# Gated cross attention and mixture of experts on one core: two x buffers, search rounds and masks placed anew between the shared units, and low weight parts of the first pieces made on TensorE

## What is computed

```python
# attention part
Q, K = h @ Wq.T, h @ Wk.T                         # h = ctx
sim = einsum('bhnd,bhmd->bnm', Q, K) / (sqrt(32) * 4)
thr = the 153rd largest value of each row of sim
A = sigmoid(sim) * (sim >= thr); A = (A + A.T) / 2
x = x + tanh(g0) * ((1 - gamma) * layernorm(x) + gamma * A)
# feed-forward part
n = layernorm(x)
shared = silu(n @ gate.T) * (n @ value.T) @ down.T        # 704 hidden columns
scores = sigmoid(n @ gate_w.T); the 2 best of 8 experts by scores + bias, weights normalised
out = x + tanh(g1) * (shared + sum over the two experts of w_e * expert_e(n))   # 352 hidden columns each
```

## Time and profile before

| | |
|---|---|
| median of 3 runs | 589.0 us |
| profiled execution | 588.87 us |
| its span, first to last instruction | 587.1 us |
| PE busy | 494.9 us (84%) |
| DVE, ACT, POOL busy | 343.4, 263.1, 231.5 us |
| mean granted TensorE clock | 0.934 of full speed |
| granted clock from 25 to 50 us, and from 50 to 75 us | 0.51 and 0.64 |

### The profile page before, as it was taken

The page is one execution under the profiler, slowest core; times in us unless marked ns, Lnnn a source line. Parts: engine busy times, 40 slices in busy tenths (PEclk is TensorE's granted clock), DMA queues, the critical chain, the costliest instruction groups (busy, mean ns, idle before and its releaser), DMA issues.

```text
span 587.1 us, 10965 instructions
## 1 busy us (share of the span) xinstructions
PE 494.9 (84%) x3105; PEld 275.4 (47%) x3106; DVE 343.4 (58%) x708; ACT 263.1 (45%) x473; POOL 231.5 (39%) x226
## 2 busy tenths in 40 slices
PE   2402588879996999778998899999999999999992
PEld 0100343334442444334464566666666666666661
DVE  0589758787868796977993577433333333333331
ACT  1696578736784569524141265322223223222221
POOL 2147835463344524470133034433443443443422
PEclk9855769989998999896999999999999999999998
DMA  3236293204720482025005589454454355345333
GB/s 117 95 85 181 79 303 118 58 18 172 263 57 19 143 291 58 20 73 185 1 0 157 189 222 258 89 91 89 73 88 91 71 82 96 72 78 98 73 40 49
DMA packets 32048, 63.73 MB, mean 109 GB/s; under 512 B 4048, under 2 KB 4304, under 8 KB 32016
## 3 DMA queue, kind: packets, MB, share of 16 engines
q1 hardware_dynamic: 23280, 42.89, 22.5%
q0 software_dynamic: 8736, 20.45, 19.3%
HBM read 41.05 MB, written 22.28 MB: 108 GB/s over the span
## 4 chain that ended last, share of the span: by engine, by line
PE 56%; DVE 18%; ACT 9%; issue 7%; DMA 5%; POOL 2%; SPq 1%; DVEq 1%; POOLq 0%; ACTq 0%
PE py L1021 13%; PE pg L1001 12%; PE pu L1002 12%; PE pg L860 4%; PE pu L860 4%; PE pt_bank L818 4%; DVE w L1195 3%; DVE pa L1154 3%; DVE w L1125 2%; PE pa L1011 2%; ACT w L627 2%; ACT w L633 2%; PE pu L880 1%; DVE w L1158 1%; DVE w L1202 1%
## 5 line engine op out<-in xcount | busy, mean ns | idle before, releaser
L1001 PE MATMUL pg<-w,x_t 128*128 x468 | 140.7, 313 | 0.0
L1002 PE MATMUL pu<-w,x_t 128*128 x468 | 140.7, 313 | 0.0
L555 POOL DMA_INDIRECT out<-rows,idx x39 | 61.8, 1584 | 141.5 <-ACT rows L758 131.4
L1021 PE MATMUL py<-w,work 128*128 x351 | 82.1, 379 | 0.8 <-DVE work L1453 0.8
L860 PE MATMUL pg<-w 128*128 128x512 f16 x288 | 78.2, 388 | 2.4 <-DVE work L1249 2.4
L748 ACT ACTIVATE work<-pg 128x352 f32<-128x352 f32 x39 | 18.1, 464 | 132.1 <-PE pu L1002 132.1
L860 PE MATMUL pu<-w 128*128 128x512 f16 x240 | 66.7, 388 | 0.0
L594 ACT ACTIVATE w<-stage 128x544 f16<-128x544 f32 (+1 forms) x80 | 50.8, 648 | 34.3 <-DMA stage<-in_weights 33.8
L496 POOL TENSOR_TENSOR w<-stage,w 128x544 f16<-128x544 f32 (+1 forms) x43 | 53.5, 1254 | 27.2 <-ACT stage L598 25.3
L1442 DVE SCALAR_TENSOR_TENSOR work<-pu,work 128x352 f32<-128x352 f32 x39 | 20.5, 525 | 62.6 <-ACT work L748 62.5
L1001 PEld LDWEIGHTS pg<-w,x_t 128*128 128x128 f16 x468 | 45.8, 98 | 20.5 <-issue 0.6
(11 more groups left out here) (199 smaller groups left out, 800.4 us busy)
## 6 DMA issues: line engine op xcount, KB each, us to landing
stage<-in_weights SPq DMA_DIRECT2D x80, 272.0 KB, 3.6
w<-in_x SPq DMA_DIRECT2D x4, 1024.0 KB, 6.8
out<-w SPq DMA_DIRECT2D x16, 256.0 KB, 2.8
xn_rows<-w SPq DMA_DIRECT2D x16, 256.0 KB, 4.9
out<-rows SPq DMA_DIRECT2D x13, 256.0 KB, 3.2
rows<-out SPq DMA_DIRECT2D x12, 256.0 KB, 3.3
w<-in_ctx_t SPq DMA_DIRECT2D x4, 256.0 KB, 3.5
out<-rows,idx POOLq DMA_INDIRECT x39, 4.8
```

The source lines that it names most:

```text
L555: pool.indirect_dma_start(out=out, out_offset=bass.IndirectOffsetOnAxis(ap=idx[:, t:t + 1], axis=0), in_=rows[:, t % 2, :], in_offset=None ...
L1001: pe.matmul(pg[p][:, 0:H], lhs, w[:, item, half, at:at + H], start=begin, stop=end)
L1002: mm = pe.matmul(pu[p][:, 0:H], lhs, w[:, item, half, at + H:at + 2 * H], start=begin, stop=end)
L1021: mm = pe.matmul(py[:, :], hid_t[:, p, part * JC + j, :], w[:, item, half, at:at + C], start=(j, part, half) == (0, 0, 0), stop=(j, part) ...
```

## The change

All of these are made together.

- **Two x buffers** (`xbs`), one for even and one for odd batches, and a buffer `kept` for the masked scores, all in the space of weight item 6. The new x stays in its buffer until the shared rows are added; the store and reload of x are gone.
- **x in one step.** ACT's `base` and POOL's adds are gone. DVE does x = x * gain + kept (scalar_tensor_tensor, four per batch) and then adds the transpose and the shift in one instruction.
- **Masks** are written without waiting for the missed counts, behind the products of units 3 and 4; the check (`check`) follows unit 5's. `a_made` counts batches instead of tiles.
- **Search.** Rounds 0, 1 and 2 are issued ahead of unit 0's product, and round 3 behind it; x statistics move from before the search to behind unit 2's product (for batch 0 ahead of the score statistics).
- **Low parts on TensorE.** For pieces 0 to 5 PE multiplies the stage slot with `W_SCALE` times the identity and the high part with minus the identity, in two halves of 272 columns, and ACT copies each half out of PSUM.
- **Pieces.** 10 pieces are made before the rows of batch 0, the other shared and first expert pieces in slots behind the units: 0, 1, 2, 2, 2, 3 of them in each period and 2, 2, 2, 2 behind units 0 to 3 of the last batch. POOL makes the low parts of pieces 6 to 47, DVE those of the late ones. The shared weights lie in flat order (groups, then down parts), and in batch 0 each unit waits only for the pieces that it reads.
- **Rows.** Statistics and row scalars go by halves of two tiles. ACT copies turned tiles 1 and 3, behind tanh; DVE copies 0 and 2, behind the four score statistics and a shared row. For batch 0, ACT writes the high part directly and DVE makes the exact row itself.
- The loops over periods are unrolled.

```diff
-BEFORE = 3
-FIRST = 14
-BY_DVE = 20
+BY_PE = 6
+FIRST = 10
+SLOT_PIECES = (0, 1, 2, 2, 2, 3)
+PER_PERIOD = sum(SLOT_PIECES)
+LAST_PIECES = (2, 2, 2, 2, 0, 0)
...
-        xb = attn_tiles()
+        beside = w[:, EARLY - 1, :, :].rearrange("p b c -> p (b c)").bitcast(F32)
+        xbs = [beside[:, 0:TPB * SEQ].rearrange("p (i c) -> p i c", i=TPB), attn_tiles()]
+        kept = beside[:, TPB * SEQ:2 * TPB * SEQ].rearrange("p (i c) -> p i c", i=TPB)
...
             def together(b, more):
-                base_scalars(b + 1)
+                slots = period_pieces(b)
                 for u in range(UPS):
+                    if u == TPB - 1:
+                        base_scalars(b + 1)
                     shared_low(b, u)
-                    if u < TPB:
-                        low_piece(b + BEFORE, u)
-                add_attention(b + 1)
-                for n in range(TPB, CHUNKS - 2):
-                    low_piece(b + BEFORE, n)
-                row_scalars(b + 1)
-                for n in range(CHUNKS - 2, CHUNKS):
-                    low_piece(b + BEFORE, n)
+                    for piece in slots[u]:
+                        low_piece(*piece)
+                row_scalars(b + 1, 0)
+                row_scalars(b + 1, 1)
...
             for u in range(UPS):
                 shared_low(BATCHES - 1, u)
+                for piece in period_pieces(BATCHES - 1)[u]:
+                    low_piece(*piece)
...
+            def low_from_banks(k):
+                at = k % CHUNKS * CHUNK_W
+                for half in range(2):
+                    after(act, low_mm, k * 2 + half + 1)
+                    act.activation(w[:, k // CHUNKS, 1, at + half * HALF_W:at + (half + 1) * HALF_W],
+                                   low_banks[low_pair(k)][half][:, 0:HALF_W], ACT.Copy).then_inc(w_lo[k % RING] if half else low_sb, 1)
...
-            def scores_and_rows(b, more, pieces=()):
-                if more:
+            def scores_and_rows(b, more):
+                if more and b:
                     keep_qk(b + 1)
-                for k in pieces:
-                    high_piece(k // CHUNKS, k % CHUNKS)
                 for i in range(TPB):
                     normalised(b, i)
                 if more:
                     keep_scores(b + 1)
-                after(act, up_mm, b * UPS)
-                after(act, xt_mm, (b + 1) * TPB)
-                act.activation(x_tb[:, :, (TPB - 1) * P:], xt_banks[(TPB - 1) % 2], ACT.Copy).then_inc(xt_act, 1)
-                if more:
                     score_tanh(b + 1)
+                rows_turned(b, 1)
+                rows_turned(b, 3)
...
             def together(b, more):
+                slots = period_pieces(b)
                 count(b + 1, 0)
                 keep_logits(b)
+                count(b + 1, 1)
                 for u in range(UPS):
                     shared_silu(b, u)
-                    if u + 1 < ROUNDS:
-                        count(b + 1, u + 1)
...
+                    if u == 0:
+                        count(b + 1, 2)
+                    if u in (1, 2):
+                        scaled_sigmoid(b + 1, 2 * u - 2)
+                        scaled_sigmoid(b + 1, 2 * u - 1)
+                    shared_high(b, u)
+                    if u == 0:
+                        count(b + 1, 3)
+                    for piece in slots[u]:
+                        high_piece(*piece)
...
+            def low_pieces(begin, end):
+                for k in range(begin, end):
+                    at = k % CHUNKS * CHUNK_W
+                    after(pe, w_hi, k + 1)
+                    for half in range(2):
...
+                        pe.matmul(bank_[:, 0:HALF_W], scaled_ident[:], stage[:, k % RING, lo:hi], start=True, stop=False)
+                        pe.matmul(bank_[:, 0:HALF_W], minus_ident[:], w[:, k // CHUNKS, 0, at + lo:at + hi],
+                                  start=False, stop=True).then_inc(low_mm, 1)
...
             pe.wait_ge(const_ok, 2)
+            low_pieces(0, RING)
             missed_rows(0)
+            after(pe, w_lo[RING - 1], 1)
+            turn_attention(0)
             project(1, None)
-            turn_attention(0)
+            low_pieces(RING, RING + 1)
             for i in range(TPB):
                 scores(1, i)
+            low_pieces(RING + 1, BY_PE)
             for i in range(TPB):
                 turn_batch(0, i)
-            for s in w_lo:
-                after(pe, s, HALVES * (CHUNKS // RING))
-            after(pe, w_hi, HALVES * CHUNKS)
...
+                after(dve, base_ok, b + 1)
+                for i in range(TPB):
+                    o.mark(dve.scalar_tensor_tensor(out=xbs[b % 2][:, i, :], in0=xbs[b % 2][:, i, :], scalar=pt[:, 4, i:i + 1],
+                                                    in1=kept[:, i, :], op0=ALU.mult, op1=ALU.add))
                 if shared is not None:
                     shared_rows(shared, 0)
                 for i in range(TPB):
-                    after(dve, xa_made, b * TPB + i + 1)
                     after(dve, at_mm, b * TPB + i + 1)
-                    dve.tensor_tensor(xb[:, i, :], turn_banks[i][:, :], xb[:, i, :], ALU.add).then_inc(x1_made, 1)
+                    o.wait()
+                    dve.scalar_tensor_tensor(out=xbs[b % 2][:, i, :], in0=turn_banks[i][:, :], scalar=pt[:, 5, i:i + 1],
+                                             in1=xbs[b % 2][:, i, :], op0=ALU.add, op1=ALU.add).then_inc(x1_made, 1)
...
             def together(b, more):
+                search(b + 1, 0)
+                if b:
+                    shared_rows(b - 1, TPB - 1)
+                search(b + 1, 1)
+                search(b + 1, 2)
+                shared_hidden(b, 0)
+                search(b + 1, 3)
+                last_counts(b + 1, (0, 1))
+                shared_hidden(b, 1)
+                thresholds(b + 1, (0, 1))
+                last_counts(b + 1, (2, 3))
+                thresholds(b + 1, (2, 3))
+                shared_hidden(b, 2)
                 x_stats(b + 1)
-                search(b + 1, 0)
...
+                shared_hidden(b, 3)
+                count_missed()
+                masks(b + 1, (0, 1))
+                shared_hidden(b, 4)
+                masks(b + 1, (2, 3))
+                shared_hidden(b, 5)
+                check(b + 1)
                 attended(b + 1, more, b)
```

More of the change, by code:

```diff
@@ L502, in shared_low @@
                 if u == MIXED:
+                    for n, low in enumerate(w_lo):
+                        after(pool, low, len(range(n, pieces_by(b, u), RING)))
                     after(pool, hlo_sb, q)
@@ new lines, in low_rows @@
+                def low_rows(i, made):
+                    after(dve, xn_hi, b * TPB + i + 1)
+                    if made is not None:
+                        o.wait(made)
+                    dve.tensor_tensor(xnr[:, i, C:2 * C], xn[:, i % 2, :], xnr[:, i, 0:C], ALU.subtract).then_inc(xn_lo, 1)
+                for i in (0, 2):
+                    if i and b == 0:
+                        after(dve, xn_lo, b * TPB + i)
+                    made = [exact(i), exact(i + 1)] if b == 0 else [None, None]
+                    low_rows(i, made[0])
+                    low_rows(i + 1, made[1])
@@ L1235, in attended @@
-                if more:
-                    score_stats(b + 1, (2, 3))
+                    rows_turned(b, 0)
+                    rows_turned(b, 2)
+                    if not more:
+                        shared_rows(shared, 3)
                 o.clear()
```

475 lines of the change are left out of this document (232 added, 243 removed).

## The result

The changed kernel takes 586.2 us (median of 8 runs, 583.9 to 587.5), the kernel before beside it 589.1 (588.4 to 591.1): the ratio on record, from all runs side by side, is 0.9937, 95% interval 0.9915 to 0.9958 (the two medians alone give 0.9951). It is faster by 0.5 to 0.6%, where 595.0, slower by 1%, had been forecast. The profiled execution took 586.68 us with a span of 584.8, 2.3 less than before.

The account below looks back on a forecast made before the run. PE carries 56% of the chain that ended last, with its waits for vector work on the path. The sum was 588.9 - 3.6 (front) + 0 (period 0) + 2.2 (period 1) + 2.4 (period 2) + 5.1 (last batch) = 595.0 us, range 582 to 602.

Parts of the forecast that it names:

- front: Before unit 0 of batch 0: earlier attention, most of it lost again behind low products and piece loads; 3.6 us gained.
- period 0: Batch 0's unit 0 to batch 1's: PE waits 6.4 us for a low piece before down products; 0 in the sum.
- period 1: Unit 0 of batch 1 to that of batch 2: middle gains 1 us, tail costs more; 2.2 us longer.
- period 2: Unit 0 of batch 2 to that of batch 3: normalising at 51.8 us, low clock in last down product; 2.4 longer.
- last batch: Unit 0 of batch 3 to the experts: eight Pool pieces hold DVE's one-hot work, partly covered by slack; 5.1 us longer.
- experts: Expert tiles at the end of the kernel: their 258 us are not touched, no term in the sum.
- the middle of periods 1 and 2: Unit 0 to normalising: masks leave PE's path, four x instructions join; normalising at 50.3 against 51.3 us, 1 us gained.
- The hold: Running Pool instructions delay DVE's four two-input x instructions, each by 1.15 us: 6.8 us instead of 2.6 free.
- The tail: Normalising to next unit 0: turned-tile copies stand behind score work; 12.4 to 13.0 us against 10.5, cost 2 to 2.5.
- rival 1: Periods gain because Pool's pieces miss the four x instructions, shown by new x by 41 us; 581 to 585, chance 0.22.
- rival 2: Last batch's hold mostly missed, as Pool's pieces fall on reductions and PSUM reads; 588 to 590.5 us, chance 0.14.
- the forecast's own 592 to 599: Whole kernel slower by the last batch's hold and the longer tail; chance 0.52.

Follow-up runs that it names:

- e10: e7 with Pool clearing instead of subtracting the low part of the seven pieces beside units 3 to 5 of each period: 575.2 us, ratio 0.9751.
- e2: Changed kernel with turned tiles copied ahead of tanh (ACT) and ahead of and between the score statistics (DVE): 581.6 us, ratio 0.9842.
- e1: Changed kernel with Pool's subtraction for the last batch's eight pieces replaced by a memset, leaving out item 5's low weights: 579.2 us, ratio 0.9798.
- e4: Changed kernel with batch 0's wait for all 16 shared pieces before the first down product replaced by a wait per unit: 579.8 us, ratio 0.9802.
- e9: Changed kernel with pieces 0 to 5 made by ACT and Pool as before the change, without identity products on PE: 583.4 us, ratio 0.9895.
- e3: Changed kernel with Pool's three subtractions of each period's last slot moved behind the row scalars: 590.0 us, ratio 0.9976.
- e5: Changed kernel with the masks of batches 1 to 3 behind the check again, ahead of the x scaling: 592.8 us, ratio 1.0053.
- e6: Changed kernel with the edits of e2, e3 and e4 together: 580.3 us, ratio 0.9848.
- e7: Changed kernel with the edits of e2 and e4 together, Pool's pieces not moved: 579.7 us, ratio 0.9838.
- e8: e7 with six of the last batch's eight pieces moved into the three periods: 575.5 us, ratio 0.9742.

## Why the prediction went wrong, step by step

The terms of the sum against the stage table, in us against the kernel before:

| term | predicted | measured |
|---|---|---|
| front | -3.6 | -4.7 |
| period 0 | 0 | -0.1 |
| period 1 | +2.2 | -1.3 |
| period 2 | +2.4 | -1.4 |
| last batch | +5.1 | +4.7 |
| experts | 0 | +0.6 |
| sum | +6.1 | -2.3 |

**The step that failed is the middle of periods 1 and 2.** The two terms were 3.5 and 3.8 us too high, 7.3 of the 8.4 that the sum missed. They made a loss of 2.2 and 2.4 us out of what became a gain of 1.3 and 1.4, and with it the sign of the whole. The mechanism was as told, its sizes were not.

- Period 1, in us behind the start of its unit 0: the x instructions start at 35.6 (predicted 36.7) and take 5.6 (6.8); the new x starts at 41.8 (44.2); ACT normalises at 47.4 (190.00 in the trace) where 50.3 was said. The hold was priced at 4.2 us over the free 2.6, as if each of the four met a Pool instruction; it is 3.0, which is three at 1.6 us and one free at 0.74 (the row below has both prices), and e10 took 1.95 of it away. The 1.1 us of the start is a chain ahead of unit 2's product that was placed 1.2 us too late (20.6 measured, 21.8 told). The rows behind the new x took another 0.5 us less than said.

```profile
L1260 DVE SCALAR_TENSOR_TENSOR w<-w,pt x16: 739/1602/1702, 48.9 to 243.2; 128x512 f32<-128x512 f32 x16
```

- The tail is a small part of it: 13.1 us where 12.4 to 13.8 was said, but the sum went by 13.8, 0.7 us too many, with a PE wait of 1.96 us before the third turned tile (1.7 to 3.8). Only e2 showed how much of it could be had back.
- Period 2 was given 51.8 us to the normalising, 1.5 more than period 1, without a row behind it; it took 48.0.

The transposes stood at 40.4 us as predicted (40.1). So the condition of rival 1, the new x by 41 us into the period, came within 0.8 us of being met: part of its gain was there, and the time, 586.2, lies between that rival (581 to 585) and rival 2 (588 to 590.5), clear of the forecast's own 592 to 599.

**What was right.** The last batch: 4.7 us against 5.1. DVE's work on the slots ended 45.2 us after unit 0's start, 6.9 later than before (8.8 predicted), and PE's slack took 2.3 of that (3.7 predicted): both were told too large, and that the sum came so close is in part luck. e1 shows the cause. Period 0: a wait of 6.04 us for a piece (6.4 predicted), a sum of zero. That the wait could be had back cheaply was not seen: the down products need the last pieces one after another (e4). The front: transposes at 48.9 (49.5 predicted), normalising at 65.2 (66.6), unit 0 at 75.6 (76.6), with the scatter of the start, up to 2.4 us, in each of them. Behind the first count the front gained 2.9 us, so the 3.6 forecast is not shown to better than that scatter.

**The rule for the hold.** The prediction held only DVE instructions with two SBUF inputs. Beside a subtraction the TENSOR_SCALAR above, with one, took 1.19 us instead of 0.17. It is one instruction in the last batch, so the sum hardly feels it.

**What was told as a gain and is a loss.** The prediction put the whole front on one account. It named the chain from a low product through the stage slot of piece 9 to the normalising, but took it as the price of an earlier attention. e9 shows that the account splits: the pieces on TensorE bring the attention 2.3 us sooner and unit 0 2.9 us later. The front's gain must stem from what remains: x's statistics beside the projections, four rounds close together, and masks beside an idle Pool. The masks' median fell from 1725 to 753 ns; line 1215, all sixteen:

```profile
L1215 DVE SCALAR_TENSOR_TENSOR w<-w,thr x16: 746/753/1705, 44.8 to 234.2; 128x512 f32<-128x512 f32 x16
```

**What stays open.** How much of the front's gain is x's statistics and how much the masks was not separated. That kernels with the same wait differ in the clock behind it is shown, why is not.

## What to carry to other kernels

Price a contended instruction by what its neighbour engine does just there: ask for each instruction of a row whether the other is busy, not for the row. Where a period is one chain round four engines, a gain in its middle is only worth what the next wait leaves of it, so after every edit read what PE waits for at the start of the period; here one row moved ahead of four statistics gave as much as the change as a whole (0.6 points of the ratio each). And a wait on "all the pieces" ahead of work that needs them one by one costs its length and the clock behind it.

## What the runs showed of the hardware that was not expected

- Behind the same PE wait of 2.17 to 2.18 us in the last batch, the same 24 products took 2.90 us after the change and in e3, e4, e5 and e9, and 4.25, 5.41, 4.60 and 3.98 in e2, e6, e7 and e10; with no wait ahead of them (e8) they took 2.90. A wait of 2 us therefore costs 0 to 2.5 us of clock here, and kernels that differ only elsewhere get different prices: all four slow ones have the edited tail, none of the five others has it.
- A clear of 128x544 on Pool takes 0.55 us and held no DVE instruction with two SBUF operands in the last batch (e1), where the subtraction of the same size takes 1.21 to 1.67 us and holds them. One TENSOR_SCALAR of 1x39 with a single SBUF operand was held by both: 0.17 us alone, 0.46 beside the clear, 1.19 beside the subtraction.
- Pool is held as well: the same subtraction takes 1.21 us alone and up to 1.67 beside DVE.
